# Attention scores of a fused image kernel: two float32r parts on half of the array rows in place of three bf16 parts on all of them

## The reference, cut to what matters

```python
x_in = conv1x1(x, W_in) + b_in
q = conv3x3(x_in, Wq[0], pad=1)      # 32 x 32 pixels: 1024 queries
k = conv3x3(x_in, Wk[0], pad=0)      # 30 x 30 pixels: 900 keys
v = conv3x3(x_in, Wv[0], pad=0)
for each of 4 heads of 8 channels:
    a = softmax(q_h^T k_h, over the 900 keys)
    o_h = a v_h
gates = tanh and sigmoid of proj(o) + a term of the window sums + bias
x = x + conv1x1(cell and output gate, W_out)
```

## Time and profile before

| | |
|---|---|
| median of 3 runs | 351.98 us (349.85 to 353.33) |
| the profiled execution, its own time | 355.27 us |
| its span, first to last instruction | 353.3 us |
| mean granted clock | 0.936 |
| TensorE busy | 314.1 us (89%) |
| VectorE busy | 218.1 us (62%) |
| ScalarE busy | 176.2 us (50%) |
| GpSimd busy | 35.6 us (10%) |

### The profile page before, as it was taken

One profiled execution on the slowest core, in us unless ns is written; L12 is line 12 of the kernel. 1 busy time (PEld: TensorE's weight loads), 2 busy tenths in 40 slices (PEclk: granted clock), 3 DMA queues, 4 the chain that ended last, 5 costly groups with the idle time before them and its releaser, 6 DMA issues. The chain is left out here.

```text
span 353.3 us, 6973 instructions
## 1 busy us (share of the span) xinstructions
PE 314.1 (89%) x2780; PEld 119.5 (34%) x2787; DVE 218.1 (62%) x484; ACT 176.2 (50%) x338; POOL 35.6 (10%) x42
## 2 busy tenths in 40 slices
PE   5899887999845799999999999999998998895894
PEld 2578332334211222332323233233331222443831
DVE  3990435674845228686878868887773123489945
ACT  1210110251833658787888878879786684300000
POOL 8300000100000000100101001010100105306000
PEclk9999999999955569999999999999998899999999
DMA  7100000037875313003030030000000000000001
GB/s 243 42 4 4 12 0 3 0 86 193 160 93 152 113 45 122 0 3 120 2 100 21 3 120 2 1 2 2 1 2 1 1 2 0 0 2 1 4 2 59
DMA packets 4043, 15.21 MB, mean 43 GB/s; under 512 B 955, under 2 KB 1771, under 8 KB 3083
## 3 DMA queue, kind: packets, MB, share of 16 engines
q1 hardware_dynamic: 4011, 14.76, 15.4%
HBM read 12.21 MB, written 2.37 MB: 41 GB/s over the span
## 5 line engine op out<-in xcount | busy, mean ns | idle before, releaser
L677 ACT ACTIVATE arena_b<-ps 128x512 f32<-128x512 f32 x232 | 125.4, 605 | 41.6 <-PE ps L1164 40.6
L1140 PE MATMUL ps<-arena_a 72*128 72x450 bf16 x256 | 90.2, 384 | 6.2 <-issue 4.7
L1164 PE MATMUL ps<-arena_a 75*128 75x512 bf16 x224 | 87.1, 400 | 7.3 <-DMA arena_a<-mt_sb 6.5
L884 DVE TENSOR_REDUCE mx<-ps 128x1 f32<-128x450 f32 x120 | 69.2, 617 | 6.7 <-PE ps L1140 5.7
L879 DVE CUSTOM_DVE_ANT_0 sums<-ps,relus 128x450 bf16<-128x450 f32 x68 | 41.6, 625 | 46.6 <-PE ps L1140 35.8
L1182 PE MATMUL ps<-arena_b,vt 128*32 128x512 f32 x448 | 62.8, 634 | 0.5 <-ACT arena_b L677 0.4
L1164 PEld LDWEIGHTS ps<-arena_a 75*128 75x128 bf16 x224 | 22.0, 100 | 81.6 <-ACT arena_b L677 44.8
L685 ACT ACTIVATE relus<-ps 128x450 f32<-128x450 f32 x68 | 37.3, 551 | 11.5 <-PE ps L1140 11.5
L1140 PEld LDWEIGHTS ps<-arena_a 72*128 72x128 bf16 x256 | 24.5, 102 | 41.5 <-issue 12.7
L1031 PE MATMUL ps<-arena_a,cst 32*32 32x512 f32 x864 | 28.6, 596 | 1.3 <-ACT arena_a L628 1.3
L1001 PE MATMUL ps<-zeros 128*128 128x512 bf16 x82 | 21.3, 398 | 6.7 <-DMA xa<-x 3.8
(11 more groups left out here) (139 smaller groups left out, 229.3 us busy)
## 6 DMA issues: line engine op xcount, KB each, us to landing
arena_b<-wmodes SPq DMA_DIRECT2D x4, 1024.0 KB, 4.9
arena_a<-k_scratch SPq DMA_DIRECT2D x3, 516.8 KB
arena_a<-q_scratch SPq DMA_DIRECT2D x3, 384.0 KB
cst<-consts SPq DMA_DIRECT2D x1, 1045.0 KB, 9.0
k_scratch<-arena_b SPq DMA_DIRECT2D x3, 344.5 KB, 3.8
cst<-consts SPq DMA_DIRECT2D x1, 864.5 KB, 6.9
arena_a<-k_scratch SPq DMA_DIRECT2D x6, 129.2 KB
arena_a<-k_scratch SPq DMA_DIRECT2D x3, 258.4 KB
```

Source lines behind the costliest of these rows:

```text
L677: nc.scalar.activation(probs[:, n % PRING, :], ps[:, SCORE_RING[n % len(SCORE_RING)], :], ACT.Exp).then_inc(expd, 1)
L884: nc.vector.tensor_reduce(mx[:, a, e:e + 1], bank, AX.X, ALU.max).then_inc(max_read, 1)
L1140: mm(ps[:, block_bank(i), 0:KHALF], qst[0:PAIR_ROWS, e, g, qt * P:(qt + 1) * P], kst[0:PAIR_ROWS, g, at:at + KHALF], start=True, stop=True ...
L1164: last = mm(ps[:, bank, :], kst[0:S_ROWS, g, t * P:(t + 1) * P], qst[0:S_ROWS, e, g, :], start=True, stop=True)
```

## The change

- q and k are split in two parts of type float32r (`PARTS = 2`). All four part products take 4 x 8 = 32 rows. A pattern row (zero in k) and the rows of the maximum's two parts follow, so max blocks have 33 rows and score tiles 35. Two heads share a slot: head 2j on rows 0 to 63, head 2j + 1 on rows 64 to 127. The order of the max blocks alternates between the two, and the types are zipped.
- The stacks of image 0 no longer go through DRAM: eight "replicas" (two products of a selection matrix with the parts, 32 rows) bring them to PSUM, and ScalarE (k ranges 0 and 1) and VectorE (q, k range 2) copy them out. Images 1 to 3 and all second query halves still go through DRAM, now in 4-byte words.
- The q stacks (8 DMAs each) and the DMAs of the maxima (2 per half) are issued by GpSimd; SyncE keeps the k stacks and the writes. Two DMAs bring a pattern to the extra rows of k, two bring zeros to rows 32 to 63 of each half in q. GpSimd also makes the rest tiles' keys (`krest`), with two products of 128 rows for a rest tile in place of four.
- The list begins right after the k convolution and the first q half. The second q half, the v convolution and the transposes of v stand in it, each followed by two entries of the stream; the window products stand further down.
- A step is `s0 X s1 X s2 X V0 s3 X V1`: the values go in two groups of 256 queries. The rate is 4.5 entries per step, 16 entries stand ahead, only half 0 is all pairs, the ring of max blocks has 4 banks and that of the values' sums one.
- VectorE's split of a maximum has three operations where it had five. The warm-up has 16 bf16 products and no others.

```diff
-KPAD = DT * P + 32
-KDIFF = KPAD
-KW = KPAD + KHALF
-K_RANGES = (slice(0, KPAD), slice(KDIFF, KW))
-PARTS = 3
-PAIR_ROWS = PARTS * PARTS * HC
-S_ROWS = PAIR_ROWS + PARTS
+KDIFF = KEYS
+KW = KEYS + KHALF
+K_RANGES = (slice(0, KHALF), slice(KDIFF, KW), slice(KHALF, KEYS))
+PARTS = 2
 HALF_TILES = HALF // P
+SLOTS = G // 2
+ROW_TILE = P // 2
+STACK = PARTS * PARTS * HC
+M_ROW = STACK + 1
+MAX_ROWS = STACK + 1
+S_ROWS = M_ROW + PARTS
...
-MAX_RING = (3, 4, 5)
-O_RING = (6, 7)
+MAX_RING = (3, 4, 5, 6)
+O_RING = (7,)
+XIN_BANKS = (0, 1, 2, 6, 3, 4, 5, 7)
...
-FIRST_AHEAD = 18
-WIDE_AHEAD = 12
-BLOCKS_PER_STEP = 4.15
+FIRST_AHEAD = 16
+BLOCKS_PER_STEP = 4.5
+STEP = 's0 X s1 X s2 X V0 s3 X V1'
+REST_STEP = 's0 X V'
 MOVED = 4
+REPLICAS = [(what, j, n, engine) for j in range(2)
+            for what, n, engine in (("k", 0, "act"), ("q", 0, "dve"), ("k", 1, "act"), ("k", 2, "dve"))]
+ORDER_OF_MAX = [(2 * j + u) * HALF_TILES + qt for j in range(2) for qt in range(HALF_TILES) for u in range(2)]
+WINDOW_AT = {(2, 5): "mean", (2, 9): "value", (2, 13): "gate"}
+PAIRED = (0, 3, 6)
+INTERLEAVE = True
...
+    for r in REPLICAS[:4]:
+        put("replica", *r)
+    group = []
     for s in range(2 * B):
-        for a in range(ROWS_OF_MAX):
-            pair = s < 2 or a % 8 in (0, 3, 6)
-            for kind in (("diff", "first") if pair else ("first", "second")):
-                stream.append(("max", i, s, a, kind))
-                i += 1
+        for p, a in enumerate(ORDER_OF_MAX):
+            if s == 0 and p == 4:
+                for r in REPLICAS[4:]:
+                    put("replica", *r)
+            kinds = ("diff", "first") if s < 1 or p % 8 in PAIRED else ("first", "second")
+            group.append([("max", s, a, kind) for kind in kinds])
+            if p % 2:
+                for items in (zip(*group) if INTERLEAVE else group):
+                    for item in items:
+                        put(*item)
+                group = []
+            if (s, p) in WINDOW_AT:
+                put("window", WINDOW_AT[(s, p)])
...
+    early = [("conv", "q", 1, px) for px in range(3)] + [("qsplit",)]
+    early += [("conv", "v", e, px) for e in range(2) for px in range(3)] + [("vcopy",), ("vt", 0), ("vt", 1)]
+    take(4 + 2)
+    for item in early:
+        plan.append(item)
+        take(2)
+    take(len(REPLICAS) + 2 * ROWS_OF_MAX + 1 + FIRST_AHEAD - 6 - 2 * len(early))
...
+        qst = over(base_a, "qst", 0, [2, SLOTS, HALF])
+        kst = over(base_a, "kst", G * HALF, [SLOTS, KW])
...
+            zero_words = HALF // 2
+            for u in range(2):
+                r0 = ROW_TILE * u + STACK
+                sp.dma_start(qst_f.rearrange("p e s n -> p (e s n)")[r0:r0 + 32, 2 * HALF:].rearrange(
+                    "p (a n) -> p a n", n=zero_words), zeros[r0:r0 + 32, :].bitcast(F32).unsqueeze(1).to_broadcast(
+                        [32, (G - 2) * 2, zero_words])).then_inc(pattern_in, 16)
...
+            def stack_k(i, s0, s1):
+                for u in range(2):
+                    for v in range(PARTS):
+                        r0 = ROW_TILE * u + PARTS * HC * v
+                        src = k_dram.rearrange("t c (s u) n -> u (t c) s n", u=2)[u][:, s0:s1]
+                        sp.dma_start(kst_f[r0:r0 + PARTS * HC, s0:s1, :], src).then_inc(k_in[i], 16)
+            sp.wait_ge(k_high, 3)
+            sp.dma_start(k_dram[0].rearrange("c g n -> g c n"), kparts_f[:, 0, 0:KW]).then_inc(kd_written, 16)
+            sp.wait_ge(k_low, 3)
+            sp.dma_start(k_dram[1].rearrange("c g n -> g c n"), kparts_f[:, 1, 0:KW]).then_inc(kd_written, 16)
+            for v, ready in enumerate((q_high, q_low)):
+                sp.wait_ge(ready, 1)
+                sp.dma_start(q_dram[v, 0].rearrange("c g n -> g c n"), qparts_f[:, v, 0:HALF]).then_inc(qd_written[0], 16)
             sp.wait_ge(kd_written, PARTS * 16)
-            stack_k(0, 0, HEADS // 2)
-            sp.wait_ge(qd_written[0], PARTS * 16)
-            stack_q(0, 0, 0, HEADS)
-            stack_k(1, HEADS // 2, HEADS)
-            stack_k(2, HEADS, 2 * HEADS)
-            stack_q(1, 0, HEADS, 2 * HEADS)
-            stack_k(3, 2 * HEADS, G)
-            stack_q(2, 0, 2 * HEADS, G)
-            for s in range(PARTS):
-                sp.wait_ge(q_part[s], 2)
-                sp.dma_start(q_dram[s, 1].rearrange("c g n -> g c n"), q_parts[:, s, HALF:HW]
-                             ).then_inc(qd_written[1], 16)
-            for s in range(2 * B):
-                e, b = divmod(s, B)
-                sp.wait_ge(*blocks_read[turn_of[s]])
-                sp.dma_start(qst[PAIR_ROWS:S_ROWS, e, b * HEADS:(b + 1) * HEADS, :].rearrange("p g n -> p (g n)"),
-                             mt_sb[:]).then_inc(m_in, 16)
-                if s == 0:
-                    sp.wait_ge(qd_written[1], PARTS * 16)
-                    stack_q(3, 1, 0, G)
-                if s == 1:
-                    sp.wait_ge(ones_in, 16)
-                if 1 <= s <= WM_PIECES:
-                    cols = slice((s - 1) * WM_COLS, s * WM_COLS)
-                    sp.dma_start(wm[:, cols], wmodes[:, cols]).then_inc(wm_loaded, 16)
+            stack_k(0, 2, 4)
+            for v, ready in enumerate((q_high, q_low)):
+                sp.wait_ge(ready, 2)
+                sp.dma_start(q_dram[v, 1].rearrange("c g n -> g c n"), qparts_f[:, v, HALF:HW]).then_inc(qd_written[1], 16)
+            for b in range(2, B):
+                if b > 2:
+                    sp.wait_ge(m_in, 2 * 16)
+                stack_k(b - 1, 2 * b, 2 * b + 2)
...
+            def stack_q(i, e, s0, s1):
+                for u in range(2):
+                    for v in range(PARTS):
+                        src = q_dram[v, e].rearrange("c (s u) n -> u c s n", u=2)[u][:, s0:s1]
+                        for t in range(PARTS):
+                            r0 = ROW_TILE * u + HC * (PARTS * v + t)
+                            pool.dma_start(qst_f[r0:r0 + HC, e, s0:s1, :], src).then_inc(q_in[i], 16)
+            pool.wait_ge(xin_ready, 2)
+            pool.wait_ge(qd_written[0], PARTS * 16)
+            stack_q(0, 0, 2, 4)
+            stack_q(1, 0, 4, 6)
...
+                if item[0] == "turn":
+                    s = item[2]
+                    e, b = divmod(s, B)
+                    pool.wait_ge(*blocks_read[item[1]])
+                    for u in range(2):
+                        r0 = ROW_TILE * u + M_ROW
+                        n = PARTS * 2 * HALF_TILES
+                        pool.dma_start(qst_f[r0:r0 + PARTS, e, 2 * b:2 * b + 2, :].rearrange("p s n -> p (s n)"),
+                                       mt_f[n * u:n * (u + 1), :]).then_inc(m_in, 16)
+                    if s == 0:
+                        pool.wait_ge(m_in, 2 * 16)
+                        stack_q(2, 0, 6, SLOTS)
+                        pool.wait_ge(qd_written[1], PARTS * 16)
+                        stack_q(3, 1, 0, SLOTS)
+                    if 1 <= s < B:
+                        pool.wait_ge(k_in[s - 1], 4 * 16)
+                        rest_tiles(s)
...
+            def replica(i, what, j, n):
+                bank = ring_bank(i)
+                r = images[0]
+                if what == "k":
+                    pe.wait_ge(k_low, n + 1)
+                    for u in range(PARTS):
+                        last = mm(ps[:, bank, 0:KHALF], select[r, 0, j, u], kparts[r, u, K_RANGES[n]],
+                                  start=(u == 0), stop=(u == 1))
+                else:
+                    pe.wait_ge(q_low, n + 1)
+                    for v in range(PARTS):
+                        last = mm(ps[:, bank, :], select[r, 1, j, v], qparts[r, v, n * HALF:(n + 1) * HALF],
+                                  start=(v == 0), stop=(v == 1))
+                last.then_inc(max_scored, 1)
...
             def max_block(i, s, a, kind):
-                before = block_before(i, block_bank(i))
-                if before is not None:
-                    pe.wait_ge(*blocks_read[before])
+                bank = ring_bank(i)
                 e, b = divmod(s, B)
                 h, qt = divmod(a, HALF_TILES)
-                g = b * HEADS + h
+                j, u = divmod(h, 2)
+                r = slice(ROW_TILE * u, ROW_TILE * u + MAX_ROWS)
                 at = {"first": 0, "second": KHALF, "diff": KDIFF}[kind]
-                mm(ps[:, block_bank(i), 0:KHALF], qst[0:PAIR_ROWS, e, g, qt * P:(qt + 1) * P],
-                   kst[0:PAIR_ROWS, g, at:at + KHALF],
+                mm(ps[:, bank, 0:KHALF], qst[r, e, 2 * b + j, qt * P:(qt + 1) * P], kst[r, 2 * b + j, at:at + KHALF],
                    start=True, stop=True).then_inc(max_scored, 1)
...
                     t, h = divmod(i, HEADS)
-                    g = b * HEADS + h
-                    last = mm(ps[:, bank, :], kst[0:S_ROWS, g, t * P:(t + 1) * P], qst[0:S_ROWS, e, g, :],
+                    j, u = divmod(h, 2)
+                    r = slice(ROW_TILE * u, ROW_TILE * u + S_ROWS)
```

(71 more changed lines are left out.)

553 lines of the change are left out of this document (305 added, 248 removed).

## The result

Four runs of the changed kernel gave a median of 461.37 us (456.62 to 465.9), four of the kernel before on the same chip 352.65 (349.85 to 353.78): a ratio of 1.3053, 95% interval 1.2914 to 1.3193. The change makes the kernel 31% slower. The forecast was 321 with a range of 303 to 350. The profiled execution took 461.07 us, with a mean granted clock of 0.666 where the kernel before has 0.936. Some executions of a kernel run about 1 to 2% longer than its others, at a lower granted clock; the ratios and intervals in this document leave those out, so a ratio need not be the quotient of the two medians beside it.

A forecast was written before the change was run, and what follows sets the result against it. TensorE alone bounded the score phase, with waits elsewhere. First score tile at 107 us, halves of 19.3 and a last of 20.4 put the last rest tile at 264.3, 31 us earlier: 321 us, range 303 to 350.

The forecast's parts named there:

- rival 2: Steady score phase falls to 1.2 GHz and TensorE alone bounds; 370 us at half the time; chance 0.15.
- the 19.5 us without blocks that kept 1.00: Old kernel's late stretch, 277.3 to 296.8 us: TensorE waited between steps at full clock; cited against the clock falling.
- the half: Score phase between two rest tiles: 19.3 us forecast, 17.6 to 21 around it, before 21.59.
- The split: Values in two groups per step: entering and leaving the narrow shape twice, 1.32 us in place of 1.10.
- The half at full clock: Score phase between rest tiles: TensorE 19.4, ScalarE 17.6, VectorE 17.4 us of work; 19.3 taken for the half.
- With that gone each waits on the others at times: Score phase: without TensorE's slowness covering them, engines wait on each other; nothing under 17.6 us, 19.3 taken.
- First max block: Front part: selection products in place of the way through DRAM, start at 77.3 us instead of 89.0.
- First score tile: End of the front part: start at 107 us, from 104 to 112, where before had 117.3.
- GpSimd's queue: Ahead of the first score tile: maxima's DMA behind 16 q DMAs, issue bounds 0.72 and 1.05 us each.
- rival 4: GpSimd's queue is the new wait: first tile at 112, half 1's maxima late by 4, 330 us; within the forecast's 0.54.
- Row halves beside each other, one pass for float32r, weight loads hidden: Max blocks and score tiles: one-pass products overlap across row halves, 182 ns loads just hide; 8.5 us per half.
- rival 1: Score phase: row halves don't run beside each other, for bank or weight waits; 335 to 352 us, chance 0.16.

The follow-up runs named there:

- m2_steps: TensorE's work of ten steps per form, no other engines or computation, from full clock; changed kernel's step 2.85 us, with whole values 2.09, before's 2.74.
- m3_cold: TensorE-only streams and eight steps per form, each after 9 us without work; changed kernel's step stayed at clock 0.50, before's came back some 4 us in.
- e2_filler: Changed kernel with one full bf16 product of zeros (128 rows, 512 columns) added ahead of each score tile; 556.37 us.
- f1: Changed kernel with zero rows filling each row half to 64, zeros in DMAs over 32 partitions, values still in two groups; 372.09 us.
- f2: Changed kernel with zero rows filling each row half to 64, zeros in DMAs over 32 partitions, values whole; 351.69 us, ratio 0.9876 to the kernel before.
- m1_streams: TensorE-only streams of 450-column products, each behind 28 full products, no computation; float32r 0.105 us a product with row halves in turn.
- e3: Changed kernel with zero rows filling each row half to 64, zeros in DMAs over 29 partitions, values in two groups; 447.37 us.
- e4: Changed kernel with zero rows filling each row half to 64, zeros in DMAs over 29 partitions, values whole; 440.92 us.

## Why the prediction was wrong

- **The step that failed** is the weight of rival 2: "If the steady phase falls to 1.2 GHz, TensorE's 17.4 to 19.4 doubles to some 35". Its size came out (34.7 to 38.4 us), in part by luck: I doubled a step of 2.53 us (1.32 for the values, 8.5 / 7 for the rest); at full clock a step takes 2.85 (m2_steps), and at half clock 5.02 (m3_cold), 1.76 times as much and not twice. It got a chance of 0.15, and I priced it at 370 us for half of the time at the low clock. It was nearly all of the time, and above the range. The reason I gave against it, the 19.5 us without blocks that kept 1.00, was the mistake: those steps ran on 75 rows, in bf16, and from a full clock. m3_cold and e2_filler show that keeping the clock and getting it back are two things, and f1 and f2 that the number of rows decides here whether it comes back. The term of the sum that failed is the half: 19.3 us put down, 34.7 to 38.4 measured between the rest tiles from 191.78 to 377.16. I had treated half the array rows as free room, and without them in use the clock did not come back.
- **The rule on the clock.** My reason for rival 2, a TensorE that has less to do and waits more, and the short idle times that I cited for it are not what happened: TensorE shows no idle time from 200 to 300 us at 0.50. The Trainium skill (TensorE: Matmul & The Clock Gate, Part 1: The HAM clock gate) has the full clock follow when TensorE is kept busy. The trace differs, with 100 us of 100% busy at the low clock; what a product uses of the array must come into it, and here the measurement decides.
- **The split**: forecast 0.22 per step, measured 0.76 at full clock (m2_steps), 3.8 us more per half than I took. With it TensorE's step is 2.85, more than before's 2.74: even at full clock, this form had nothing to give. The drains that I took from the trace were right (0.57 from the start of a group to the next start, before 1.00 for the whole one); what was missing is the lone pair between them.
- **The half at full clock**: 19.3 forecast. Without the split TensorE's work comes to 2.09 per step, less than I took, but f2's halves are 21.1 to 23.5. "With that gone each waits on the others at times" was right and too cheap: 1.7 us put down for it, about 4 needed.
- **First max block**: 77.3 forecast, 78.47 measured. **First score tile**: 107, measured 117.42, and 110.83 in f2, which has the half clock from 104 to 117 too. The front part gains where the clock allows it: f2's last rest tile is at 287.29, before's at 295.03, 7.7 us, and 6.5 of these are there at the first score tile. But before's profiled execution (355.27) is 3 us over its median and f2's (347.46) 4 under. By the ratio of 0.9876 f2 is 4 us ahead, and the interval ends at 1.0.
- **GpSimd's queue** (rival 4) did no harm: 16 DMAs from 84.61 on in 9.11 us, 0.57 each, below both of my bounds (0.72 and 1.05), and TensorE doesn't wait ahead of the first score tile.
- **Row halves beside each other, one pass for float32r, weight loads hidden** (rival 1 against): right, 0.105 us a product and loads of 186 ns in m1_streams.

## What to carry to other kernels

A layout that packs a product into fewer array rows can cost the clock: look at the granted clock of a stretch beside TensorE's busy share, and test a new layout from the low clock as well as from the high one, since it may keep the clock and yet never bring it back. More rows cost TensorE nothing (2.85 us a step on 64 rows as on 35 and 33, m2_steps, with data in them), and rows of zeros gave 89 us back (f1). Splitting a group of products in another shape costs the entry, the exit and whatever small work is shut in between, and here it kept the clock down for longer; measure that step alone first, from both clocks.

## What was not expected of the hardware

- The clock has a memory: bf16 on 72 rows held 1.00 for 17.3 us from a full clock, and stayed at 0.50 for 26.4 from a low one. Rows of zeros count (f1 and f2: halves near 21.6 us in place of 37.5).
- Products on one row half alone lost the clock within the stream, float32r some 3 us in (0.35 us each on average, in place of 0.21) and bf16 some 5 us in (28.56 us for 90).
- A pair of products of one row half between two groups of the narrow shape took 0.63 us, three times its price in the flow.
- The zeros of e3 and e4, two DMAs of 0.9 MB over 29 partitions each, moved at 15 to 21 GB/s and cost an 88 us wait; two of 1.0 MB over 32 partitions each landed in 12.3 us. In e4, from 110 to 150 us, the DMA engines' busy share is 0.06, as much as one of the 16 makes when it is full. Whether the number of partitions or another part of the form did it wasn't tried.
